# First norm of two quarters applied by GpSimd, and the first octet's payload gates moved ahead of a head maximum

## What is computed

```python
x = layernorm(x + self_attention(x))        # 16 heads of 8, softmax over the 32 positions
x = layernorm(x + cross_attention(x, ctx))  # softmax over the 16 heads (axis=1), not over positions
x = layernorm(x + ffn(x))                   # shared expert of 512 + top 3 of 15 routed experts of 256
# layernorm: (x - mean) / sqrt(var + 1e-5), no scale and no shift
# routing: softmax over 15 logits, the three largest weights gate their experts
```

## Time and profile before

| what | us |
|---|---|
| median of 3 executions | 285.23 (285.05 to 285.29) |
| the profiled execution, its own time | 285.98 |
| span of the profiled execution, first to last instruction | 284.1 |
| PE busy in the span | 230.8 |
| DVE busy | 220.7 |
| ACT busy | 190.7 |
| POOL busy | 183.3 |

### The profile page before, as it was taken

The page is one execution under the profiler, slowest core; times in us unless marked ns, Lnnn a source line. Parts: engine busy times, 40 slices in busy tenths (PEclk is TensorE's granted clock), DMA queues, the critical chain, the costliest instruction groups (busy, mean ns, idle before and its releaser), DMA issues.

```text
span 284.1 us, 7099 instructions
## 1 busy us (share of the span) xinstructions
PE 230.8 (81%) x2283; PEld 175.7 (62%) x2283; DVE 220.7 (78%) x613; ACT 190.7 (67%) x420; POOL 183.3 (65%) x170
## 2 busy tenths in 40 slices
PE   7988999887799788659957889975898996989840
PEld 3777777675554344334524466665698996978830
DVE  7775999997999999999995579724164673878784
ACT  4597998754798589767645755425177784777663
POOL 7043474443047584589896877777767777777874
PEclk9999999998999979988989799999599998999995
DMA  6694471012500000049603115351424437375464
GB/s 184 248 254 93 87 220 42 6 38 75 150 0 2 0 0 2 14 115 367 227 30 121 47 52 146 102 127 57 115 68 123 115 94 220 104 214 139 155 198 139
DMA packets 38597, 31.90 MB, mean 112 GB/s; under 512 B 12864, under 2 KB 31552, under 8 KB 38432
## 3 DMA queue, kind: packets, MB, share of 16 engines
q1 hardware_dynamic: 34608, 23.90, 30.0%
q0 software_dynamic: 3520, 7.27, 7.5%
q10 hardware_dynamic: 432, 0.27, 0.3%
HBM read 19.95 MB, written 11.47 MB: 111 GB/s over the span
## 4 chain that ended last, share of the span: by engine, by line
DVE 36%; PE 23%; issue 16%; POOL 11%; DMA 8%; ACT 3%; SPq 2%; DVEq 1%; POOLq 0%; ACTq 0%
POOL x_srt L1954 9%; DVE prob_sums L1493 7%; PE psum L983 5%; DVE maxes L1487 5%; DMA k_heads<-x_srt 5%; PE psum L992 4%; PE psum L569 3%; DVE prob_sums L1407 2%; PE psum L620 2%; PE psum L975 2%; PE psum L586 1%; DVE maxes L1402 1%; DVE v_rows L1478 1%; SPq L458 1%; DMA xT<-x_t 1%
## 5 line engine op out<-in xcount | busy, mean ns | idle before, releaser
L2016 POOL DMA_INDIRECT y_tok<-k_heads,y_rows x62 | 61.6, 994 | 19.9 <-issue 14.5
L1311 ACT ACTIVATE k_heads<-psum,k_heads 128x128 f32<-128x128 f32 x124 | 38.7, 363 | 35.5 <-PE psum L983 30.6
L1954 POOL DMA_INDIRECT x_srt<-v_blocks,slot x48 | 47.2, 983 | 15.4 <-issue 15.1
L1931 POOL TENSOR_TENSOR k_heads<-k_heads,inv_sums 128x1024 f32<-128x1024 f32 x16 | 30.9, 1939 | 25.2 <-DVE inv_sums L1498 25.1
L983 PE MATMUL psum<-k_heads 128*128 128x128 f32 x248 | 40.2, 286 | 3.7 <-DVE k_heads L1810 3.7
L1810 DVE COPY k_heads<-psum 128x128 f32<-128x128 f32 x62 | 17.9, 288 | 31.1 <-PE psum L975 30.0
L992 PE MATMUL psum<-k_heads 128*128 128x128 f32 x248 | 39.1, 281 | 0.3 <-ACT k_heads L1311 0.3
L983 PEld LDWEIGHTS psum<-k_heads 128*128 128x128 f32 x248 | 33.8, 198 | 5.2 <-DVE k_heads L1810 4.7
L1919 POOL TENSOR_TENSOR probs<-probs,inv_sums 128x512 f32<-128x512 f32 x16 | 16.7, 1048 | 28.3 <-DVE inv_sums L1412 28.1
L992 PEld LDWEIGHTS psum<-k_heads 128*128 128x128 f32 x248 | 33.9, 198 | 0.5 <-ACT k_heads L1311 0.5
L1794 DVE COPY k_heads<-expert_w 128x514 f32 x62 | 27.2, 444 | 3.4 <-issue 2.6
(11 more groups left out here) (189 smaller groups left out, 524.3 us busy)
## 6 DMA issues: line engine op xcount, KB each, us to landing
expert_w<-e_w SPq DMA_DIRECT2D x1, 4369.0 KB, 16.0
k_heads<-x_srt SPq DMA_DIRECT2D x62, 65.0 KB
q_heads<-y_tok SPq DMA_DIRECT2D x8, 256.0 KB, 3.5
x_srt<-pad SPq DMA_DIRECT2D x16, 65.0 KB
xT<-x_t SPq DMA_DIRECT2D x4, 256.0 KB, 5.8
ctxT_k<-ctx_k SPq DMA_DIRECT2D x2, 512.0 KB, 5.5
v_scr<-v_rows SPq DMA_DIRECT2D x4, 256.0 KB, 2.8
ctxT_v<-ctx_v SPq DMA_DIRECT2D x2, 512.0 KB, 5.4
```

The source lines that it names most:

```text
L1311: ins = act.activation(h_tile[:, t % 2, a, :], bank[2 + t % 2][:, P * a:P * a + P], ACT.Gelu, bias=tile_weights(t)[:, EW - 2 + a:EW - 1 + a])
L1931: pool.tensor_tensor(probs2[:, p % 3, :].rearrange("p (t h) -> p t h", t=B), probs2[:, p % 3, :].rearrange("p (t h) -> p t h", t=B), inv_s ...
L1954: pool.indirect_dma_start(out=x_srt, out_offset=bass.IndirectOffsetOnAxis(ap=slot[:, n:n + 1], axis=0), in_=payloads[:, g, k, :], in_offse ...
L2016: pool.indirect_dma_start(out=y_tok, out_offset=bass.IndirectOffsetOnAxis(ap=y_rows[:, t:t + 1].bitcast(mybir.dt.uint32), axis=0), in_=y_t ...
```

## The change

Two things are done, and neither changes the arithmetic that is carried out on a value, apart from the engine that carries it out.

First, `ln1_apply(0)` and `ln1_apply(1)` leave DVE's list and stand in POOL's: quarter 0 between `normalise(8)` and `normalise(9)`, quarter 1 between `normalise(12)` and `normalise(13)`. Each is four `tensor_scalar` instructions of 128x128 with two per-partition scalars (subtract the mean, multiply by the inverse deviation). Quarters 2 and 3 stay on DVE.

Second, `route_gates` is cut in two. The sum, the inverse and the payload gates stay in it; the kept gates become `route_kept`. For octet 0, `route_gates(0)` now stands right behind `route_slots(0)` and ahead of `head_max(10)`, and `route_kept(0)` stands behind `o_turned(1)`. For octets 1 to 3 `route_kept` follows `route_gates` at once, so their order is the old one.

```diff
@@ DVE: route_gates cut in two
                 dve.tensor_tensor(gate, route_exp[:, :, NE:NE + TOPK], lsc.unsqueeze(2).broadcast_to([P, 4, TOPK]),
                                   ALU.mult).then_inc(s_payload_gates, 1)
+
+            def route_kept(c):
+                lsc = logit_sum[:, 4 * c:4 * c + 4]
                 routed(dve.tensor_tensor(route_in[:, :, 0:NE], route_exp[:, :, 0:NE], lsc.unsqueeze(2).broadcast_to([P, 4, NE]), ALU.mult))
                 dve.tensor_tensor(gates[:, 4 * c:4 * c + 4, 0:NE], route_in[:, :, 0:NE], chosen[:, 4 * c:4 * c + 4, :],
                                   ALU.mult).then_inc(s_gates, 1)
@@ DVE's list, first stage
             turn(7)
-            ln1_apply(0)
             row_sum(9)
...
             turn(11)
-            ln1_apply(1)
             row_max(14)
@@ DVE's list, second stage
             route_slots(0)
+            route_gates(0)
             head_max(10)
-            route_gates(0)
             o_turned(1)
+            route_kept(0)
             head_sum(9)
...
             route_gates(1)
+            route_kept(1)
@@ POOL: the apply, and its two places
+            def ln1_apply(c):
+                pool.wait_ge(s_rstd1, 2 * (c + 1))
+                for j in range(4):
+                    pool.tensor_scalar(x1_pre[:, c % 2, j, :], x1_pre[:, c % 2, j, :], mean_var1[:, c % 2, j, 0:1],
+                                       rstd1[:, c % 2, j:j + 1], ALU.subtract, ALU.mult).then_inc(s_x1, 1)
...
             normalise(8)
+            ln1_apply(0)
             normalise(9)
...
             normalise(12)
+            ln1_apply(1)
             normalise(13)
```

More of the change, by code:

```diff
@@ L1736, in _ @@
             route_gates(2)
+            route_kept(2)
             route_slots(2)
@@ L1739, in _ @@
             route_gates(3)
+            route_kept(3)
             route_slots(3)
```

## The result

The changed kernel is slower. Its median is 287.35 us over 20 executions (285.13 to 290.56), against 285.63 (283.57 to 287.82) for 20 executions of the kernel before, and the ratio is 1.0064 with a 95% interval of 1.0043 to 1.0086. The forecast was 283.9. Each ratio is worked out from the undisturbed executions alone, the medians from all of them, so the two need not agree to the last digit (here the medians give 1.0060). The profiled execution has a span of 286.4, where the kernel before had 284.1.

The account below looks back on a forecast made before the run. No engine fills the span; DVE is fullest in the first stage, DVE and POOL nearly full from 118 to 150 us. Gains of 1.15 and 0.2 gave 285.23 - 1.35 = 283.9 us, range 282.9 to 285.3.

Parts of the forecast that it names:

- What bounds the kernel: First stage, 36 to 64 us: DVE fullest at 27.28 of 28.00, PE and ACT not far behind.
- the forecast of the first part: First stage: moving eight applies from DVE to POOL gives 1.15 us.
- The price A of a set of applies on POOL: Four 128x128 applies on POOL, first stage: taken as 1.55 us, between 0.92 and 2.2.
- upper bound: POOL's four applies: 2.2 us at most, from the dearest 512 elements (1.29) plus four times 0.23.
- The prediction's own sign of being wrong: First stage, POOL: the forecast is wrong if one apply takes over 0.55 us; two other signs concerned the gates.
- The arithmetic around A: First-stage waits worked out by set price: 1.15 us gained at 1.55, about 0.7 left at 2.2.
- break-even at `turn(9)`: DVE's `turn(9)`, behind `normalise(9)`: nothing gained here if a set on POOL takes 1.98 us.
- POOL becomes the bound of the first stage: Rival, chance 0.10: fixed software cost per apply on POOL; at 3.2 us a set, 1.0 slower in all, 286.2.
- point of decision: `turn(13)`, began at 59.18: all gain gone at 2.6 us a set, each further 0.1 costs 0.2.
- PE's transposes of quarter 1: PE, first stage: they come later than the applies end (55.9), so they are not held.
- The second part: Octet 0's payload gates ahead of `head_max(10)`: held by `normalise2(8)`, first scatter earlier, 0.2 us gained.
- Nothing behind 150 us takes the gain back: After the second stage: scatters and tiles follow in fixed distances, no transfer starts at a fixed time, so gains last.

Follow-up runs that it names:

- e10: Kernel before with quarters 0 and 1 applied on POOL as two wide products each, quarter 0 behind `normalise(9)`, gates unmoved: 284.41 us against 285.8, ratio 0.9974.
- e3: Kernel before plus ten extra POOL instructions behind `rsqrt1(3)`, pricing six forms of an apply; nothing left out: one execution, 287.7 us.
- e8: Changed kernel with the gates in their old place and each POOL set of applies as two wide products: ratio 0.9923 to the kernel before.
- e1: Changed kernel with the gates put back in their old place, applies of quarters 0 and 1 on POOL: 287.09 us against 285.92, ratio 1.0054.
- e4: Kernel before with only quarter 0's applies on POOL, behind `normalise(8)`; quarter 1 on DVE, gates unmoved: 287.97 us against 285.92, ratio 1.0058.
- e6: Kernel before with the gates moved and octet 0's inverse sum in PSUM, applies on DVE: ratio 1.0027, repeated 0.9998.
- e2: Kernel before with only the gates moved as in the changed kernel, all applies on DVE: 285.41 us against 285.92, ratio 0.9972.
- e5r: Repeat run: kernel before with only quarter 0's four applies on POOL, behind `normalise(9)`; gates unmoved: 284.54 us against 285.8, ratio 0.9969.
- e9r: Repeat run: kernel before with wide-product applies on POOL, quarter 0 behind `normalise(9)`, gates moved, inverse sum in PSUM: 283.3 us against 285.8, ratio 0.9955.

## Why the prediction was wrong

**What bounds the kernel** held. DVE was the fullest engine of the first stage, and relieving it can be worth time: e10 gained 1.20 us there. That the forecast of the first part was 1.15 confirms no number, since e10 has the first set elsewhere and in another form.

**The price A of a set of applies on POOL is the step that failed.** It was taken as 1.55 with an upper bound of 2.2, and it measured 3.14. The working drew a line through two products of 512 and 1024 elements: 1.72 ns an element, 0.17 fixed. Both numbers were wrong for this instruction. The prices of e3 give 3.4 ns an element and 0.36 fixed, paid four times. Some 0.17 of an apply goes to its two per-partition scalars; what makes the rest dear no run takes apart. Even the plain product of 128 elements takes 0.55 to 0.71, not 0.39. The upper bound was made of rows as unlike the apply as the lower one was, so it bounded nothing. The prediction's own sign of being wrong, an apply over 0.55, came: 0.79. The range, 282.9 to 285.3, inherited that and left the slower case out.

The Trainium skill's rule, in GPSIMD Engine Reference, section 4.1, that one-input work on GpSimd runs roughly at line rate, doesn't hold for these rows: DVE took 1.07 for the set, POOL 3.14.

**The arithmetic around A was right**, with its place as well as its slope. It put break-even at `turn(9)` at A = 1.98. With 3.14 it gives 1.16 late; the trace has 1.12 (5.23 behind `normalise(8)` instead of 4.11). With A = 2.2 it left "about 0.7" of the gain; e8, at 2.19, has 0.79.

**What happened is the rival "POOL becomes the bound of the first stage".** It had a chance of 0.10 and forecast 1.2 later at A = 3.2; the first stage is 1.08 longer. Its point of decision, `turn(13)`, was right too. By its formula `normalise(13)` ends at 55.97 + (3.14 - 1.98) + 3.14 = 60.27, and `turn(13)`, 59.18 before, is 1.1 late. Counted from the first `ln1_added`, `normalise(13)` ends at 21.26 in e1 and at 21.23 in the changed kernel, and `turn(13)` starts at 21.29 in both, 1.03 later than before (20.26).

It looks otherwise in e4, where the first set alone costs the same. There DVE still has the second set, never makes up for the late `turn(9)`, and `turn(13)` comes 1.12 late behind DVE's own work (21.38); `normalise(13)` had ended 0.80 earlier. In e1 DVE does make up for it: `row_sum(14)` is only 0.12 later than before (19.53 instead of 19.41), and then `turn(13)` waits for POOL. (In the changed kernel the dip of the clock makes DVE itself late, so that both arrive together.) So the second set's 1.4 us of relief is real, and is lost again behind the same set on POOL. That both come to 1.1 is chance. Where a set takes 2.19, in e8, `turn(13)` doesn't wait for POOL and comes 0.80 earlier than before. One smaller step failed as well: PE's transposes of quarter 1 were to find the applies done, and in e1 the last of them waits 0.27 for POOL.

**The second part was right up to the first scatters.** Counted from the start of `normalise2(8)`, 2.09 later in this trace: `head_max(10)` at 119.36 - 2.09 = 117.27 (forecast 117.3), L1516 reached at 127.58 (127.6) and held until 128.40 (128.4), the gates held 1.10 (1.1), the first scatter 0.22 earlier (0.2). e6 shows the cause: with one operand in PSUM the same product at the same moment takes 0.18. The rule in SBUF - State Buffer, section "Who interferes with whom", of the Trainium skill, that a VectorE instruction with two SBUF inputs contends with a GpSimd instruction that reads SBUF, agrees with both numbers.

"Nothing behind 150 us takes the gain back" did not hold. In the changed kernel the wait of 0.51 shown above took it, and in e2 it is gone as well, without that wait: the last scatter starts at 80.45, in the middle of the 80.33 to 80.55 of the five kernels with the gates in their old place.

**What isn't accounted for.** The two distances give 1.08 - 0.22 = 0.86 us, or 1.08 if the second part's gain is lost, and the medians differ by 1.72, with the ratio's interval from 1.2 to 2.5. The changed kernel's runs had a mean granted clock of 0.939, those of the kernel before, beside e1, 0.946. Within the kernel before, the time falls by about 0.6 us for each 0.01 of clock, loosely, so this would be 0.4 more. That is argued, not shown, and no experiment changed the clock alone. The rest stays open.

## What to carry to other kernels

The price of an instruction form that the trace doesn't show is measured first, or bounded by its number of instructions, operations and per-partition operands; a line through other sizes of another form is no bound. Before work is moved to an idle engine, ask which of the instructions behind it somebody is waiting for: the same 3.1 us cost 1.1 in one place and gained 0.5 one place later. A short DVE product that had to run beside a long one on POOL was held until that one's end with both operands in SBUF, and was free with one of them in PSUM; whether that was worth time, the runs don't decide.

## What the runs showed of the hardware that had not been expected

On POOL, splitting this tile is dear and fusing the two operations isn't cheap: four fused `tensor_scalar` of 128x128 take 3.14, one of 128x512 takes 2.08, and two separate wide products about 2.1.

TensorE starts a run at either of two rates. The same first matmuls of 384 columns, two in each row, behind the same six warm-up matmuls, in the kernel before and in e10:

```profile
5.75 1.49 PE L539 MATMUL psum<-xT,weights 128*128 128x384 f32 x2
```

```profile
5.39 0.81 PE L540 MATMUL psum<-xT,weights 128*128 128x384 f32 x2
```

The granted clock of the stretch is shown as 1.00 in both. The next row of the same form starts 1.28 us behind this one in the first trace (7.03) and 0.64 in the second (6.03), a factor of two, so the slow start looks like the level of 1.2 GHz; what decides between them is not known. From the first projection to the first `ln1_added` the one takes 34.16 and the other 32.46. Of the fourteen profiles e2, e5r, e9r and e10 have the fast start and the other ten the slow one, in which that distance is 33.99 to 34.20. So 1.7 us between two single profiles can be chance, and a span alone does not judge a change of 1 us. The granted clock also dips at places that change from run to run: behind the first stage it was 0.67 in the kernel before, 0.57 in the changed one and 1.00 in e1, and from the last `ln1_added` to `normalise2(8)` these take 51.08, 51.44 and 49.95 us.

```profile
69.00:73.00 4.00, 3.96 (x23) 3.77 (x23) 2.71 (x6) 3.21 (x6) 0.00 (x0) 0.67 0.35 105
```

```profile
70.70:74.70 4.00, 4.00 (x22) 3.98 (x22) 2.30 (x7) 3.07 (x6) 0.00 (x0) 0.57 0.38 108
```

```profile
71.50:75.50 4.00, 3.71 (x31) 3.47 (x31) 3.68 (x9) 3.34 (x7) 0.00 (x0) 1.00 0.38 108
```
